# Where the running maximum of the scores is taken: SBUF copy or PSUM, in an attention kernel on one Trainium2 core

## The reference

```
f, g, h = Wq xn, Wk xn, Wv xn          # (64, 4096), (64, 4096), (256, 4096) per image
scores  = f^T g                        # (n, m): 4096 x 4096
beta    = softmax(scores, axis=n)      # over the rows n, for each column m
out     = x + (gamma * (h beta) + xn)
```

## Time and profile before

| | |
|---|---|
| median of 3 runs | 2040.77 us (2040.7 to 2041.21) |
| profiled execution | 2041.25 us |
| its span, first to last instruction | 2039.5 us |
| TensorE busy | 1982.0 us, 97% of the span |
| VectorE busy | 1627.3 us, 80% |
| ScalarE busy | 1610.5 us, 79% |
| GpSimd busy | 1312.3 us, 64% |
| mean granted TensorE clock | 0.996 of full speed |

### The profile page before, as it was taken

One profiled execution on the slowest core, in us unless ns is written; L12 is line 12 of the kernel. 1 busy time (PEld: TensorE's weight loads), 2 busy tenths in 40 slices (PEclk: granted clock), 3 DMA queues, 4 the chain that ended last, 5 costly groups with the idle time before them and its releaser, 6 DMA issues.

```text
span 2039.5 us, 43654 instructions
## 1 busy us (share of the span) xinstructions
PE 1982.0 (97%) x17732; PEld 1730.5 (85%) x17732; DVE 1627.3 (80%) x2208; ACT 1610.5 (79%) x1699; POOL 1312.3 (64%) x738
## 2 busy tenths in 40 slices
PE   3899999999999999999999999999999999999999
PEld 1688888888888888888888888888878888888887
DVE  8788899887867889887876888988787677777774
ACT  4588878888867887888877888788887788888885
POOL 2066667876546666887555666688655566666667
PEclk9899999999999999999999999999999999999999
DMA  2012211211102211211101121121101011111111
GB/s 95 1 32 73 71 30 42 73 29 28 23 18 70 71 43 29 72 52 22 28 21 48 42 73 48 32 63 52 29 21 27 20 30 32 22 32 30 31 22 42
DMA packets 188745, 82.68 MB, mean 41 GB/s; under 512 B 148352, under 2 KB 181376, under 8 KB 188544
## 3 DMA queue, kind: packets, MB, share of 16 engines
q1 hardware_dynamic: 188544, 79.90, 14.7%
HBM read 46.53 MB, written 16.78 MB: 31 GB/s over the span
## 4 chain that ended last, share of the span: by engine, by line
PE 90%; DVE 6%; ACT 2%; issue 1%; DMA 1%; SPq 0%; ACTq 0%; DVEq 0%
PE O L353 20%; PE O L354 20%; PE O L352 20%; PE S L338 10%; PE S L339 10%; PE O L325 1%; PE O L361 1%; PE O L327 1%; PE O L326 1%; ACT SC L452 1%; DVE SC L600 1%; DVE XM L587 1%; PE MB L371 1%; DVE gr L558 1%; DMA SC<-x 1%
## 5 line engine op out<-in xcount | busy, mean ns | idle before, releaser
L261 POOL TENSOR_TENSOR PL<-SC,PH 128x1024 f16<-128x1024 f32 x512 | 1091.6, 2135 | 690.5 <-ACT SC L459 686.5
L353 PE MATMUL O<-V,PH 128*128 128x256 f16 x4096 | 1119.5, 273 | 0.0
L352 PE MATMUL O<-V,PH 128*128 128x257 f16 x4096 | 1115.6, 272 | 2.0 <-DVE GL L608 2.0
L354 PE MATMUL O<-V,PL 128*128 128x257 f16 x4096 | 1112.9, 272 | 0.0
L452 ACT ACTIVATE SC<-S 128x1024 f32<-128x1024 f32 x512 | 523.7, 1023 | 304.2 <-PE S L339 301.5
L587 DVE TENSOR_TENSOR XM<-SC,XM 128x512 f32<-128x512 f32 x896 | 618.5, 690 | 173.8 <-ACT SC L452 160.5
L600 DVE TENSOR_TENSOR SC<-SC,MB 128x1024 f32<-128x1024 f32 x512 | 620.1, 1212 | 53.0 <-PE MB L371 52.3
L458 ACT ACTIVATE PH<-SC 128x1024 f16<-128x1024 f32 x512 | 537.8, 1050 | 25.6 <-DVE SC L600 17.3
L459 ACT ACTIVATE SC<-SC 128x1024 f32<-128x1024 f32 x512 | 536.3, 1048 | 0.0
L338 PE MATMUL S<-G,F 128*128 128x256 f16 x2048 | 477.6, 274 | 16.0 <-ACT SC L452 12.1
L339 PE MATMUL S<-GL,F 128*128 128x256 f16 x2048 | 477.7, 274 | 0.0
(11 more groups left out here) (75 smaller groups left out, 972.1 us busy)
## 6 DMA issues: line engine op xcount, KB each, us to landing
xin<-x SPq DMA_DIRECT2D x24, 1024.0 KB, 5.6
xres<-x SPq DMA_DIRECT2D x64, 256.0 KB, 2.9
out<-RES SPq DMA_DIRECT2D x64, 256.0 KB, 2.2
ATT<-OT SPq DMA_DIRECT2D x1008, 16.0 KB, 1.8
SC<-x SPq DMA_DIRECT2D x4, 1024.0 KB, 8.4
wv<-wvT SPq DMA_DIRECT2D x1, 256.0 KB, 10.3
wqk<-wqT SPq DMA_DIRECT2D x1, 64.0 KB, 10.5
wqk<-wkT SPq DMA_DIRECT2D x1, 64.0 KB, 10.4
```

What stands on the lines that cost most here:

```text
L261: pool.tensor_tensor(PL[:, s % RING, :], sc(s), PH[:, s % RING, :], ALU.subtract).then_inc(pl_ready, 1)
L352: mm(o[:, 0:C + 1], PH[:, n % RING, cols], vh, start=t == 0, stop=False)
L353: mm(o[:, 0:C], PH[:, n % RING, cols], vl, start=False, stop=False)
L354: w = mm(o[:, 0:C + 1], PL[:, n % RING, cols], vh, start=False, stop=t == T - 1)
```

## The change

VectorE no longer reads the copied scores from SBUF. It reads `S` itself in PSUM, in turn with ScalarE so that the two are never in the same bank: while ScalarE copies the first half of S, VectorE folds the second half into the maximum, then they swap. The copy becomes two instructions of 512 elements, each with its own increment of `s_stored`. The running maximum `XM` now lies in SBUF, in two copies by turns of chunks, and is also what TensorE turns; `MX` and the PSUM bank of the old `XM` go. `scores(q)` waits for both copies and both maxima of `S`. VectorE handles q = n + 16 in step n, the scores of the same step, with both halves ahead of `divide` and `subtract`; before, the second half came after `subtract` and `scale_output`.

```
 def scores(q):                                   # TensorE
     if q > 0:
-        pe.wait_ge(s_stored, q)
+        pe.wait_ge(s_stored, 2 * q)
+        pe.wait_ge(s_maxed, 2 * q)
...
 # TensorE, g == 2, before turn_maxima(k + 1, ...), which reads XM[:, c % 2, ...] instead of MX
+    if k > 0:
+        pe.wait_ge(osb_ready, MB2 * k)
...
 def store(q):                                    # ScalarE
     act.wait_ge(s_ready, q + 1)
     if q >= 2 * G:
         act.wait_ge(pl_ready, q - 2 * G + 1)
-    nc.scalar.activation(sc(q), S[:, :], ACT.Copy).then_inc(s_stored, 1)
+    nc.scalar.activation(sc(q)[:, 0:2 * M], S[:, 0:2 * M], ACT.Copy).then_inc(s_stored, 1)
+    act.wait_ge(s_maxed, 2 * q + 1)
+    nc.scalar.activation(sc(q)[:, 2 * M:4 * M], S[:, 2 * M:4 * M], ACT.Copy).then_inc(s_stored, 1)
...
-def maximum(q, half):                            # VectorE, from SC
+def maximum(q):
+    c, g = divmod(q, G)
+    xm = XM[:, c % 2, :]
+    dve.wait_ge(s_ready, q + 1)
+    if g == 0:
+        if c >= 2:
+            dve.wait_ge(mx_turned, c - 1)
+        ve.tensor_copy(xm, S[:, 2 * M:4 * M]).then_inc(s_maxed, 1)
+    else:
+        dve.wait_ge(s_maxed, 2 * q)
+        ve.tensor_tensor(xm, S[:, 2 * M:4 * M], xm, ALU.max).then_inc(s_maxed, 1)
+    dve.wait_ge(s_stored, 2 * q + 1)
+    dve.wait_ge(s_maxed, 2 * q + 1)
+    ve.tensor_tensor(xm, S[:, 0:2 * M], xm, ALU.max).then_inc(s_maxed, 1)
...
 def subtract(s):
     dve.wait_ge(mb_ready, k + 1)
+    dve.wait_ge(s_stored, 2 * (s + 1))
...
 for n in range(K * G):                           # VectorE
-    q = n + 2 * G - 1
+    q = n + 2 * G
     if q < K * G:
-        maximum(q, 0)
+        maximum(q)
     if g == 0 and k > 0:
         divide(k - 1)
     if n + SUB_LEAD < K * G:
         subtract(n + SUB_LEAD)
     if g == 0 and k > 0:
         scale_output(k - 1)
-    if q < K * G:
-        maximum(q, 1)
```

More of the change, by code:

```diff
@@ L89, in groupnorm_attention @@
         xres = sb("xres", [P, H, M], f32)
-        MX = sb("MX", [P, 2 * M], f32)
+        XM = sb("XM", [P, 2, 2 * M], f32)
         mxc = sb("mxc", [P, MB2], f32)
@@ L112, in groupnorm_attention @@
         S = ctx.enter_context(nc.psum_tensor("S", [P, GW], f32))
-        XM = ctx.enter_context(nc.psum_tensor("XM", [P, 512], f32))
         MB = ctx.enter_context(nc.psum_tensor("MB", [P, 512], f32))
@@ L361, in turn_maxima @@
                         r = nc.tensor.transpose(bank[:, m * M + half * P:m * M + (half + 1) * P],
-                                                MX[:, half * M + m * P:half * M + (m + 1) * P], ident[:, :])
+                                                XM[:, c % 2, half * M + m * P:half * M + (m + 1) * P], ident[:, :])
                 r.then_inc(mx_turned, 1)
@@ L569, in normalise @@
                 return ve.tensor_scalar(buf, buf, nmean[:, h:h + 1], nrstd[:, h:h + 1], ALU.subtract, ALU.mult)
-            def maximum(q, half):
[L573 to L585, removed]
-                else:
-                    ve.tensor_tensor(XM[:, :], part, XM[:, :], ALU.max).then_inc(s_maxed, 1)
+            def maximum(q):
[6 more added lines that the diff above has]
+                    ve.tensor_copy(xm, S[:, 2 * M:4 * M]).then_inc(s_maxed, 1)
+                else:
+                    dve.wait_ge(s_maxed, 2 * q)
[3 more added lines that the diff above has]
+                ve.tensor_tensor(xm, S[:, 0:2 * M], xm, ALU.max).then_inc(s_maxed, 1)
             def column_maxima(c, bank):
@@ L670, in _ @@
                 if i >= 3:
-                    maximum(i - 3, 0)
-                    maximum(i - 3, 1)
+                    maximum(i - 3)
             for g in range(G):
@@ L675, in _ @@
                     column_maxima(0, O[:, 0, 1, :])
-                if g < G - 1:
-                    maximum(G + g, 0)
+                maximum(G + g)
                 low_v(g, (g + 1) % 2 if g < G - 1 else 1)
-                if g < G - 1:
-                    maximum(G + g, 1)
                 if g >= G - SUB_LEAD:
```

## The result

The changed kernel takes 2145.88 us (median of four, 2145.5 to 2147.51) against 2040.99 of before measured beside it: ratio 1.0513, 95% interval 1.050 to 1.0527. It is slower, as forecast, by 104.9 us where 75 were forecast (2116); the time lies inside the stated range over all (2068 to 2155), near its upper end. It also lies 0.9 us above the forecast's own range (2085 to 2145), at the lower edge of what the harsher rival claimed (2145 to 2200).

A forecast was written before the change was run, and what follows sets the result against it. TensorE, busy 97% of the span, was taken as the bound; terms of 11.5 + 6 + 14 + 15 + 10 + 4 + 15 = 75.5 us gave a median of 2116 us, own range 2085 to 2145, over all 2068 to 2155.

The forecast's parts named there:

- harsher rival: Small operations keep full length, normalising takes 3.0, the clock falls for longer: 2145 to 2200 us, chance 0.13.
- T: Moment ScalarE starts on a full S; TensorE needs S free by T + 2.34, forecast free at T + 1.54.
- a: Spreading of the maxima: TensorE waits for the subtract of g = 3, 0.23 in 50 chunks, 11.5 us.
- b: Statistics: they delay the next maxima, so TensorE gets S late, twelve times, 6 us (3 to 10).
- c: Normalising and rounding: normalising pair at 1.7 costs no wait; ScalarE's roundings cost 1.13 twelve times, 14 us (6 to 28).
- d: Variances and inverse roots: VectorE's small operations hold S back, 4.9 more per image, three times, 15 us (-1 to +32).
- e: Clock after the six gaps at variances and roots: half clock costs 1.7 each, 10 us (0 to 20).
- f: Projections of f and g: a closed loop of 5.2 a step makes TensorE late, three times, 4 us (1 to 10).
- g: Prelude: the same loop of 5.2 a group, later groups and project_v, 15 us (8 to 22).
- the milder: Maxima and half copies overlap more tightly, roundings find slack, the clock holds: 2043 to 2085 us, chance 0.14.
- the faster one: The existing 8.6 us of waits at j = 5 and 6 vanish: about 2032 us, chance 0.04.
- no change: The lost time hides behind TensorE, as idle shares of VectorE and ScalarE suggest: chance 0.03.

The follow-up runs named there:

- run 1: Changed kernel with VectorE's subtract moved ahead of the maxima in the main loop: 2151.75 us, ratio 1.0543.
- run 9: Changed kernel with the subtract ahead of the maxima, except at step g = 6 and in steps with a projection of f and g: 2090.27 us.
- Run 3: Changed kernel with POOL making only 4 columns of its low weights in step g = 5 of the 12 normalising chunks: 2136.33 us.
- run 11: Changed kernel with reordered VectorE list, casts first, prelude's S freed by the copy, variances and roots in six pieces, roundings in two steps: 2039.4 us.
- run 4: Changed kernel with 28 matmuls into a spare PSUM bank, filling TensorE's six gaps at the variances and roots: 2135.88 us.
- run 2: Changed kernel with ScalarE's casts of F and G ahead of its second half copy of S, also in the prelude: 2145.7 us.
- run 5: Kernel before with only the running maximum in SBUF and the copy in halves, maxima still reading the copied scores: 2242.9 us.
- run 7: Kernel before with both maxima moved to the head of the step, still reading copied scores, plus TensorE's wait on the scaled output: 2139.07 us.

## Why the prediction was right, and where it was off

What carried it was right: TensorE is the bound, S must be free by T + 2.34, VectorE's maxima free it at T + 1.49, and VectorE loses its lead, so each piece of its list longer than the slack comes to lie on TensorE's path. The steps in which that happens are the ones named, with one more: step g = 0 of the very first chunk (1.0).

- **a** was mis-sized: 11.5 for 16.9. The 0.33 was right; the 0.1 that I gave back, from one row of a late S, isn't given back here: 0.338 each. That row shows a matmul 0.06 behind the end of ScalarE's copy; here TensorE waits for VectorE, and its matmul starts 0.15 behind the end of the subtract or of the second maximum, each time. Runs 1 and 9 remove exactly this term.
- **b**: 6 for 6.8, and run 9 removes it.
- **c** failed, and the step is the sentence "after the change POOL should be nearly done with the residual then. I take 1.7". It holds for the first normalising alone, which takes 0.8 to 1.0. POOL's next instruction slips in between the two, and the second waits until it is done: 3.34 and 3.5 for the pair, and 1.66 each for TensorE where nothing was forecast. I had the other price, 3.0, and put it in the range; with it the sum gives 26 (28 at the range's top) of the 35.6. The roundings' own term was 1.31 instead of 1.13; half of that is again the 0.1 given back. Run 3 bears out what the second normalising waits for, runs 9 and 11 remove both parts.
- **d** was right to 1 us, and for the reason given: the small operations took 5.1 and 6.0 us instead of 8.83 and 8.44, because POOL ran out of work. The timeline of POOL and VectorE in the kernel after:

```profile
290.76 1.46 DVE L542 TENSOR_SCALAR gmean<-gmean 128x4 f32<-128x4 f32 x1
292.26 1.20 DVE L544 COPY bm<-gmean 128x32 f32<-128x32 f32 x1
...
294.26 0.17 DVE L549 TENSOR_SCALAR gvar<-gvar 128x4 f32<-128x4 f32 x1
...
290.07 2.13 POOL L260 TENSOR_TENSOR PL<-SC,PH 128x1024 f16<-128x1024 f32 x1 [0.31 <-ACT SC L463]
292.17 1.25 POOL L279 TENSOR_TENSOR RES<-RES,ATT 128x512 f32<-128x512 f32 x1
```

  Two of them end where POOL's two instructions end (292.2 and 293.4), and from then on they take 0.2. The maxima resumed at T + 7.7 and T + 8.6, where 8.05 and 8.6 were forecast.
- **e**, 10 for 10.9, shown as cause by run 4. That the size came so near is luck in part: I had taken a third of another stretch, and with the same gaps the clock cost 9.3 in run 2, where one gap in six went free. **f**, 4 for 3.3. **g**, 15 for 18.2, or 19.2 with the first step behind it; the loop of 5.14 us a group was forecast as 5.2, and TensorE at half clock made the later groups 3.53 instead of 2.72. What a better order of the prelude would give was misjudged in run 2, and got in part in run 11.
- Of the rivals, the milder one, the faster one and no change fell. The harsher one holds the measured time by its lower edge; it was right in its second item (normalising at 3.0 or more) and wrong in its first and third (small operations at full length, a longer half clock). That maxima read from PSUM are slower did not come: 0.690 and 0.692 against 0.69.

**A price that I took for granted.** I kept the maximum at 0.69 because one operand stays in PSUM, and that was right, but I didn't see what hung on it: had the change moved XM to SBUF and left the scores there too, it would have cost 200 us (run 5). The Trainium skill has the rule, page "SBUF — State Buffer", section "Who interferes with whom": a VectorE instruction with two SBUF inputs contends with a GpSimd instruction that reads SBUF; one with at most one, outside the 2-port modes, doesn't. By that rule, the traces agree: 0.69 and 0.695 with one, 1.21 with two. The same section says that an instruction in a 2-port mode, which it says `tensor_scalar` can enter, contends too, and that whoever issues first holds the shared ports for the whole instruction. The trace agrees at the second normalising, a TENSOR_SCALAR: 2.6 us behind POOL's instruction, 0.81 where none had got in.

## What to carry to other kernels

Where one engine frees the buffer of the engine that is the bound, everything in its list between two such instructions counts as latency, however low its busy share; look for the longest piece, not for the sum. A lead that an engine has over the bound is worth time only where it is used up, so find those places (here statistics, normalising, and 14 or 16 small operations in a row) before giving the lead away. And two instructions in a row are two chances for another engine to step in between: price the second one by the other engine's longest instruction.

## What the runs showed of the hardware

- A VectorE maximum of 512 float32 elements took 0.69 us with one operand in PSUM and one in SBUF, either way round, and 1.21 on the mean (0.64 to 2.62) with both in SBUF: 1.60 where a GpSimd instruction was running at its start, 0.68 elsewhere (run 5).
- After idle times of TensorE of 3.2 to 4.1 us the granted clock fell to its lower level in all six cases of the changed kernel, but in five of six in runs 2 and 3, and in two of three after 3.15 us in run 7. After 1.15 to 1.64 us, in 24 cases, it did not. Filling most of the gap with matmuls kept it at the upper level.
- TensorE's first matmul started 0.15 us behind the end of the VectorE instruction that it waited for, and 0.06 behind a ScalarE copy.
- Of two normalisings in a row, a GpSimd instruction got in between in 12 of 12 cases in the changed kernel, and the second took 2.6 us instead of 0.8.
- A copy of 512 elements by ScalarE took 0.60 us where 1024 took 1.02, and cutting one in two cost the kernel nothing measurable.
